# Two cross-attention and expert layers on one core: z rows stored as fp16 halves and brought into columns by DMA transposes, one joined q/k weight in the second attention, and the second expert weights split earlier

## The chip, the cores and the metric

The kernel runs on one core of a Trainium2 chip. The metric is the device time of one execution in microseconds (us). TensorE is called PE here, VectorE DVE, ScalarE ACT, GpSimd POOL and SyncE SP, as in the profile.

## What is computed

The state x is 16 batches of 256 tokens of 256 values, f32. Four parts each add to it, times tanh of a gate:

- first attention: layernorm of x as 256 latents; four heads of 64; keys and values come from a context (256 rows of 192 values) and from the latents;
- first experts: logits over 8 experts, the best two by softmax, each with silu(z W1) * (z W2) W3 and an inner width of 352, and one shared expert for all tokens;
- second attention: one head, `q = z Wq + bq`, `k = ctx Wk + bk`, `v = ctx Wv + bv`, scores `q kT`, softmax, `P v`;
- second experts: best one of 8, gelu, inner width 512, biases, the result times the gate's probability.

z is the layernorm of x at each of these places. The expert products are made from fp16 halves: a number is its fp16 rounding (high) plus the fp16 rounding of what is left (low), and three products (high with high, high with low, low with high) stand for one in f32.

## The kernel before

The phases stand one after the other, with a barrier between them: constants, first attention (about 31 to 440 us), its routing tail and a table of tiles (to 482), expert stage 0 (482 to 838), second attention (838 to 1081), its table (to 1100), expert stage 1 (1100 to the end).

**Attention phases.** Each engine has its own instruction stream; they meet by semaphores alone. `over_batches` (L247) writes a software pipeline: in step n an engine works on batch n+1 ("front"), n ("core"), n-1 ("tail") and n-2 (routing). The order inside a step is written out by hand, and an engine never leaves it: an instruction that waits holds up all behind it on that engine. Some steps at both ends are written out, the rest are a loop.

`Route` (L261) is the part of both attention phases that prepares the experts. DVE makes `z_tokens` (`vector_z`, L335) into one of two buffers, PE turns it (`pe_turn`, L346), ACT copies the columns (`act_cols`), PE makes logits and prefix sums, DVE chooses experts and slots (`vector_choose`, `vector_slots`; the last result is `slot_idx`, L446), and POOL sends each row to its slot in HBM by indirect DMAs of 128 rows (`pool_scatter`, L457, L464): four for a batch in the first attention, two in the second. In the first attention SP also stores the plain rows for the shared expert. A row is 1024 bytes of f32 z; in the second attention it carries the probability, the token number and the token's x behind z.

POOL's step in the second attention (L1625) is: `pool_rstd(n-1)` (L318, L319), `fetch(n+3)` (four gathers of expert results, L1515), `rstd(n+2)` (L1620, L1621), `pool_scatter(n-2)`. DVE uses the second rstd for `x_norm` (`pre_norm`, L1770), and PE's step begins with turning that (`turn`, L1846). Steps n = 2 to 12 have both a fetch and a scatter.

PE's step there is: turn x and context of n+1, scores of n, logits of n-2, projection of q and then of k of n+1 (`project_qk`, L1858; the k part is L1868), turning of probabilities, projection of v, prefix sums, turning of z of n-1, products of n. ACT adds the biases of q and k (`bias_q_or_k`, L1653).

**Weights.** `Weights` (L180) brings the expert weights of a layer in by parts, one for each batch step of the attention before it: SP loads 256 or 352 KB and more, ACT makes the high halves (`high`, L223), DVE the low ones (`low`, L231; the `v_low` rows of the profile are its work in the second attention, L234).

**Expert stages.** Stage 0 has 103 tiles of 128 rows (71 routed, 32 shared), stage 1 has 39. `over_tiles` (L1274) writes the pipeline: in step s PE makes the first products of tile s, turns tile s+1 of z (`z_cols`, L1403) and the hidden rows of s-1 (L1410), and makes y of s-2 (L1419). The z rows come as f32 by one plain SP load of 128 KB (L1351), issued three tiles ahead into four buffers. ACT rounds the turned columns to `z_high` (L1431) and DVE subtracts for `z_low` (L1487); the first products (L1393) wait for `z_low`. ACT and DVE further make the hidden rows and their halves. In stage 0 SP stores y; in stage 1 POOL scatters it to the output.

Of the kernel before, what the change touches and what calls it, by code (L numbers as in the profile page):

```python
# [15 lines left out]
P = 128  # L16
# [11 lines left out]
F1 = 512  # L28
REG = NTOK + P
# [43 lines left out]
def program(nc, a, out):  # L73
    root = ExitStack()
    with root:
# [34 lines left out]
        with ExitStack() as l0:  # L110
# [7 lines left out]
            end_of_phase(nc, g)  # L118
            phase_experts(nc, a, g, 0)
            end_of_phase(nc, g)  # L120
        with ExitStack() as l1:
            g["v1h"] = sb("v1_high", [P, KC * E * F1], F16, l1)
            g["v1l"] = sb("v1_low", [P, KC * E * F1], F16, l1)
            g["v2h"] = sb("v2_high", [P, 4 * E * C], F16, l1)
            g["v2l"] = sb("v2_low", [P, 4 * E * C], F16, l1)
            g["b1"] = sb("b1_rows", [P, E * F1], F32, l1)
            g["b2"] = sb("b2_rows", [P, E * C], F32, l1)
# [52 lines left out]
class Weights:  # L180
# [5 lines left out]
    def __init__(self, nc, g, a, c, layer):  # L186
        self.g, self.layer = g, layer
        if layer == 0:
            self.parts, self.first_rows, self.second_rows = 2 * (E + 1), a["w13"], a["w2"]
            self.F, self.EW, names = 2 * F0, E + 1, ("w13h", "w13l", "w2h", "w2l")  # L190
        else:
            self.parts, self.first_rows, self.second_rows = 2 * E, a["v1"], a["v2"]
            self.F, self.EW, names = F1, E, ("v1h", "v1l", "v2h", "v2l")
        self.first_rows = self.first_rows.rearrange("e c f -> (e c) f")
        self.second_rows = self.second_rows.rearrange("e f c -> (e f) c")
        self.high1, self.low1, self.high2, self.low2 = (g[x][:] for x in names)
        self.stage1 = [c.enter_context(nc.sbuf_tensor(f"w{layer}_stage_first{p}", [P, self.F], F32)) for p in range(2)]
        self.stage2 = [c.enter_context(nc.sbuf_tensor(f"w{layer}_stage_second{p}", [P, 2 * C], F32)) for p in range(2)]
        sem = lambda n: phase_semaphore(nc, g, f"w{layer}_{n}")
# [3 lines left out]
        if layer == 0:  # L203
            self.second = [[(0, P, 0, 0)], [(P, P, 1, 0), (2 * P, F0 - 2 * P, 2, 1)]]
        else:
            self.second = [[(0, P, 0, 0), (P, P, 1, 1)], [(2 * P, P, 2, 0), (3 * P, P, 3, 1)]]
# [8 lines left out]
    def load(self, sp, j, q):  # L215
        sp.wait_ge(self.low_done, count(j - 1))
        inner = F0 if self.layer == 0 else F1
        sp.dma_start(self.stage1[q][:], self.first_rows[ds(j * P, P), :]).then_inc(self.landed[q], 16)
        for row, rows, _, place in self.second[q]:
            sp.dma_start(self.stage2[q][0:rows, place * C:(place + 1) * C],  # L220
                         self.second_rows[ds((j - q) * (inner // 2) + row, rows), :]).then_inc(self.landed[q], 16)
# [9 lines left out]
    def low(self, v, j, q):  # L231
# [3 lines left out]
        ins.then_inc(self.low_done, 1)  # L235

# [24 lines left out]
class Route:  # L261
# [6 lines left out]
    def __init__(self, nc, g, c, tag, K, SL, PR, RUN, rows, wg):  # L268
# [19 lines left out]
        self.z = [sb(f"z_tokens{p}", [P, T, rows.shape[1]]) for p in range(2)]  # L288
# [4 lines left out]
        self.z_turned = sem("z_turned")  # L293
        if K == 1:
# [40 lines left out]
    def vector_z(self, v, n, p, x, shared):  # L335
# [3 lines left out]
        v.wait_ge(self.scattered[p], count((n - p) * (8 * self.K * T)))  # L339
        if shared:  # L340
            v.wait_ge(self.stored[p], count((n - p) * 8))
        for t in range(T):
            ins = v.tensor_scalar(self.z[p][:, t, 0:C], x[:, t, :], self.mv[:, t, 0:1], self.rstd[:, t:t + 1], ALU.subtract, ALU.mult)
        ins.then_inc(self.z_ready, 1)

    def pe_turn(self, pe, n, p, bank):  # L346
        pe.wait_ge(self.z_ready, n + 1)
        for k in range(KC):
            for t in range(T):
                ins = pe.transpose(bank[:, k, t * P:(t + 1) * P], self.z[p][:, t, k * P:(k + 1) * P], self.g["ident"][:])  # L350
# [63 lines left out]
    def vector_slots(self, v, n, p, prefix, beside=None):  # L414
# [13 lines left out]
        if self.K == 1:  # L428
            ch.mark(v.tensor_scalar(self.z[p][:, :, SCALE], self.sum[:], self.g["gate"][:, 3:4], None, ALU.mult))
            ch.mark(v.tensor_copy(self.z[p][:, :, NUMBER], self.number[:]))  # L430
# [19 lines left out]
    def act_tokens(self, act, n, p):  # L450
# [4 lines left out]
        act.activation(self.z[p][:, :, TOKEN:TOKEN + C], self.g["XR"][:, ds(n * T, T), :], ACT.Copy).then_inc(self.tokens_copied, 1)  # L455
# [104 lines left out]
def phase_attn0(nc, a, g):  # L560

    NS1 = DC - P
    with ExitStack() as c:
# [33 lines left out]
        xo = sb("x_mid", [P, T, C])  # L597
# [10 lines left out]
        weights, table, dummies_padded = Weights(nc, g, a, c, 0), Table(nc, g, c, 0, [x[:].rearrange("p j s -> p (j s)") for x in (pm[0], pm[1], ksq)]), sem("dummies_padded")  # L608
# [25 lines left out]
        with nc.Block() as block:  # L634
            @block.sync
            def _(sp):
# [6 lines left out]
                def store(m, p):  # L643
                    sp.wait_ge(rt.z_ready, m + 1)
                    sp.dma_start(g["z0"][ds(m * S + SHARED, S), :].rearrange("(t p) c -> p t c", p=P), rt.z[p][:]).then_inc(rt.stored[p], 16)

                def step(n, q):
# [4 lines left out]
                    if isinstance(n, int) and n == -3:  # L652
                        for dst, src in loads:
                            sp.dma_start(dst, src).then_inc(consts_in, 16)
                    if within(n - 1, B):
# [1316 lines left out]
```

## Time and profile before

| | |
|---|---|
| time, median of 3 runs | 1256.4 us (1250.9 to 1256.54) |
| the profiled execution | 1255.76 us, span 1253.9 us |
| busy: PE, DVE, ACT, POOL | 1113.0 (89%), 765.0 (61%), 600.4 (48%), 412.0 (33%) us |
| mean granted clock of PE | 0.94 of full speed |

The share of each engine is a mean over phases with different limits. PE is the busiest, but the records of weight loads overlap it, and in POOL's busy time are the indirect DMAs that it issues. A row of windows has, in order: the window, its length, busy time and (instructions) of PE, of PE's weight loads, of DVE, ACT and POOL, the granted clock, the busy share of the DMA engines, and GB/s. A row of a timeline has start, busy time, engine, line, operation, output and inputs; in brackets stand the engine's idle time just before it and what ended that.

### The profile page before, as it was taken

What the parts mean: (1) busy time and instruction counts of PE and PEld (TensorE: products, weight loads), DVE (VectorE), ACT (ScalarE), POOL (GpSimd) and SP (SyncE); (2) the same over time, 40 slices, a digit from 0 to 9 for tenths busy, and PEclk for the clock granted to TensorE, in tenths of its full rate; (3) what the DMA queues carried; (4) which work ended last, traced back from release to release, by engine and by line L of the source; (5) the groups of instructions that cost most, each with busy time, mean ns of one, the idle gap of its engine ahead of it and who ended that gap; (6) DMA issues with size and microseconds to landing.
All of it is one profiled execution on the core that took longest, in us unless ns stands there. A gap on an engine that the chain in (4) does not pass through costs nothing. (4 is left out here: it accounts for less than half of the span.)

```text
span 1253.9 us, 31159 instructions
## 1 busy us (share of the span) xinstructions
PE 1113.0 (89%) x8451; PEld 859.0 (69%) x8452; DVE 765.0 (61%) x2494; ACT 600.4 (48%) x1400; POOL 412.0 (33%) x485
## 2 busy tenths in 40 slices
PE   3999999999999944999999999965999998289996
PEld 2677777777777733777777777744777777256664
DVE  5467777777777662344444444434788887447775
ACT  3466665666566521444444444422555555033442
POOL 3345555556465430000000000004566662212222
PEclk9799999999999866999999999986999999579999
DMA  4123121311221112222222222225764541433341
GB/s 132 32 66 101 57 69 56 101 63 55 67 82 50 45 64 71 74 79 79 79 79 79 78 79 78 79 81 156 269 192 155 165 151 59 118 89 106 109 110 52
DMA packets 94382, 116.21 MB, mean 93 GB/s; under 512 B 12479, under 2 KB 80049, under 8 KB 94066
## 3 DMA queue, kind: packets, MB, share of 16 engines
q1 hardware_dynamic: 82594, 84.50, 22.1%
q0 software_dynamic: 10576, 29.41, 6.7%
q10 hardware_dynamic: 1152, 1.58, 0.5%
q8 instruction: 28, 0.46, 0.1%
q14 instruction: 32, 0.26, 0.1%
HBM read 70.43 MB, written 45.92 MB: 93 GB/s over the span
## 5 line engine op out<-in xcount | busy, mean ns | idle before, releaser
L1487 DVE TENSOR_TENSOR e_z_low<-e_z_cols,e_z_high 128x256 f16<-128x256 f32 x142 | 59.9, 422 | 209.5 <-ACT e_z_high L1431 209.2
L1431 ACT ACTIVATE e_z_high<-e_z_cols 128x256 f16<-128x256 f32 x142 | 54.5, 384 | 254.8 <-PE e_z_cols L1403 254.8
L1128 PE MATMUL a_out<-a_v_ones,a_probs 128*128 128x65 f32 x1024 | 140.6, 281 | 0.0
L1128 PEld LDWEIGHTS a_out<-a_v_ones,a_probs 128*128 128x128 f32 x1024 | 126.8, 195 | 15.3 <-issue 15.3
L464 POOL DMA_INDIRECT z_rows<-r_z_tokens,r_slot_idx x96 | 96.4, 1004 | 75.8 <-ACT r_z_tokens L455 35.7
L1608 POOL IOTA a_first_numbers<- 128x2 int32 x1 | 0.1, 125 | 367.7 <-POOLq L69 367.7
L772 ACT ACTIVATE a_probs<-a_scores,a_latent_bias,a_k_scales 128x256 f32<-128x256 f32 x128 | 65.3, 561 | 94.5 <-PE a_scores L1114 57.1
L1497 DVE TENSOR_TENSOR e_hidden_low<-e_hidden_cols,e_hidden_high 128x384 f16<-128x384 f32 (+1 forms) x142 | 83.6, 588 | 36.8 <-ACT e_hidden_high L1446 36.7
L1393 PE MATMUL e_first<-w_high,e_z_high 128*128 x412 | 96.6, 316 | 4.2 <-DVE e_z_low L1487 3.5
L1393 PE MATMUL e_first<-w_low,e_z_high 128*128 x412 | 96.3, 316 | 0.0
L1393 PE MATMUL e_first<-w_high,e_z_low 128*128 x412 | 96.3, 316 | 0.0
L1403 PE MATMUL e_z_cols<-ident,e_z_rows 128*128 128x128 f32 x284 | 55.6, 278 | 39.5 <-DMA e_z_rows<-z_rows 39.5
L1419 PE MATMUL e_y<-w_high,e_hidden_high 128*128 (+1 forms) x309 | 84.4, 273 | 2.1 <-DVE e_hidden_low L1497 1.8
L1419 PE MATMUL e_y<-w_high,e_hidden_low 128*128 (+1 forms) x309 | 84.1, 272 | 0.0
L1419 PE MATMUL e_y<-w_low,e_hidden_high 128*128 (+1 forms) x309 | 84.0, 272 | 0.0
L1373 POOL DMA_INDIRECT out_x<-e_y_rows,e_token_numbers x39 | 38.4, 984 | 126.7 <-DVE e_y_rows L1510 123.4
L1515 POOL DMA_INDIRECT a_y_chosen<-y_rows,a_slots x64 | 66.2, 1034 | 39.6 <-issue 22.9
L1403 PEld LDWEIGHTS e_z_cols<-ident,e_z_rows 128*128 128x128 f32 x284 | 40.4, 144 | 54.2 <-DMA e_z_rows<-z_rows 39.7
L1410 PE MATMUL e_hidden_cols<-ident,e_hidden 128*128 128x128 f32 (+1 forms) x465 | 74.5, 274 | 1.3 <-ACT e_hidden L1441 0.9
L695 POOL TENSOR_TENSOR a_k_scales<-a_square_sums,minus_half 128x16 f32<-128x16 f32 x16 | 46.4, 2901 | 87.7 <-DVEq L924 87.7
L1446 ACT ACTIVATE e_hidden_high<-e_hidden_cols 128x384 f16<-128x384 f32 (+1 forms) x142 | 73.8, 520 | 0.9 <-PE e_hidden_cols L1410 0.9
L772 ACT ACTIVATE a_probs<-a_scores,a_mask_bias,a_k_scales 128x256 f32<-128x256 f32 x128 | 65.4, 568 | 8.5 <-PE a_scores L1114 5.1
(339 smaller groups left out, 3083.3 us busy)
## 6 DMA issues: line engine op xcount, KB each, us to landing
e_z_rows<-z_rows SPq DMA_DIRECT2D x142, 128.0 KB, 2.0
y_rows<-e_y_rows SPq DMA_DIRECT2D x103, 128.0 KB, 1.7
w_stage_first<-in_w SPq DMA_DIRECT2D x18, 352.0 KB
a_ctx_in<-in_ctx SPq DMA_DIRECT2D x32, 192.0 KB, 3.7
e_token_rows<-z_rows SPq DMA_DIRECT2D x39, 129.0 KB, 2.1
residual<-in_x SPq DMA_DIRECT2D x16, 256.0 KB, 3.6
z_rows<-r_z_tokens SPq DMA_DIRECT2D x16, 256.0 KB, 2.2
a_y_shared<-y_rows SPq DMA_DIRECT2D x16, 256.0 KB, 2.8
```

Of the source, the lines that this page charges most:

```text
L464: pool.indirect_dma_start(self.rows, bass.IndirectOffsetOnAxis(ap=self.idx[p][:, k, t:t + 1], axis=0), self.z[p][:, t, :], None).then_inc( ...
L772: act.activation(pm[x][:, jt, :], SC[x][:, 0:S], ACT.Exp, bias=b, scale=rr[p][:, jt * 4 + h:jt * 4 + h + 1]).then_inc(exps, 1)
L1128: ins = pe.matmul(O[t][:, h * (D + 1):(h + 1) * (D + 1)], pm[x][:, jt, t * P:(t + 1) * P], va[p][:, jt, h, :], start=i + x == 0, stop=i + ...
L1393: ins = pe.matmul(GU[p][f][:, 0:F], x[p][:, k, :], w[:, ds(off, F)], start=(k == 0 and x is xh and w is wh), stop=(k == KC - 1 and x is xl))
L1403: ins = pe.transpose(ZT[:, k * P:(k + 1) * P], zs[z][:, k * P:(k + 1) * P], g["ident"][:])
L1410: ins = pe.transpose(HT[p % NH][0:m, n * P:(n + 1) * P], hs[p][:, o:o + m], g["ident"][:])
L1419: ins = pe.matmul(Y[p][:, 0:C], x[p][0:m, n, :], w[0:m, ds(e * C + n * EW * C, C)], start=(n == 0 and x is hh and w is uh), stop=(n == NCH ...
L1431: act.activation(xh[p][:].rearrange("p k s -> p (k s)"), ZT[:, 0:KC * P], ACT.Copy).then_inc(zhigh, 1)
L1446: act.activation(hh[p][:].rearrange("p k s -> p (k s)"), HT[p % NH][:, 0:HW], ACT.Copy).then_inc(hhigh, 1)
L1487: v.tensor_tensor(xl[p][:].rearrange("p k s -> p (k s)"), ZT[:, 0:KC * P], xh[p][:].rearrange("p k s -> p (k s)"), ALU.subtract).then_inc( ...
L1497: v.tensor_tensor(hl[p][:].rearrange("p k s -> p (k s)"), HT[p % NH][:, 0:HW], hh[p][:].rearrange("p k s -> p (k s)"), ALU.subtract).then_ ...
L1515: pool.indirect_dma_start(dst, None, rows, bass.IndirectOffsetOnAxis(ap=idx[:, k, t:t + 1], axis=0)).then_inc(done, 16)
```

## The change

1. z is made in one f32 buffer. ACT makes the fp16 high half (`act_z_high`, two instructions of 128x256 for a batch), POOL the low half (`pool_z_low`, two of 128x256). Both go into `zrow`, 1024 bytes for a row as before, and the scatters and stores send that. `act_z_high` stands behind the last exps in the first attention, behind `act_cols` in the second; `pool_z_low` is the last of POOL's step. `vector_z` waits for the turn and the low half of the batch before, `pool_scatter` and the store wait for the low half. In the first attention SP's store goes behind the load of weights.
2. In both expert stages SP's load becomes a DMA transpose of 128 rows x 512 fp16 into four 128x128 blocks. PE's turning, ACT's `z_high` and DVE's `z_low` go; the first products wait for the landing alone, and the load waits for the first products of four tiles before.
3. The weights of stage 1 are split in stage 0, 64 pieces of 128x256, one with each of the tiles 12 to 75 (SP a load of 128 KB, ACT one instruction, DVE one); `over_tiles` gets a second loop and more written-out steps. The second attention has none of it any more.
4. At the start of the second attention PE makes Wq WkT and its column for bk once. In the loop the k projection and its biases go; q's columns are 128 + 65 rows, scores contract them with the context's columns, which have two buffers now.
5. The first attention loses one buffer (`x_mid`); the work is the same.

```diff
-    def vector_z(self, v, n, p, x, shared):
+    def vector_z(self, v, n, x):
         v.wait_ge(self.rstd_ready, n + 1)
-        v.wait_ge(self.scattered[p], count((n - p) * (8 * self.K * T)))
+        v.wait_ge(self.z_turned, count(n))
+        v.wait_ge(self.z_low, count(n))
+        for t in range(T):
+            ins = v.tensor_scalar(self.z[:, t, :], x[:, t, :], self.mv[:, t, 0:1], self.rstd[:, t:t + 1], ALU.subtract, ALU.mult)
...
+    def act_z_high(self, act, n, p, shared):
+        act.wait_ge(self.scattered[p], count((n - p) * (8 * self.K * T)))
...
+        act.wait_ge(self.z_ready, n + 1)
         for t in range(T):
+            ins = act.activation(self.zhalf[p][t][:, 0:C], self.z[:, t, :], ACT.Copy)
+        ins.then_inc(self.z_high, 1)
+    def pool_z_low(self, pool, n, p):
+        pool.wait_ge(self.z_high, n + 1)
+        for t in range(T):
+            ins = pool.tensor_tensor(self.zhalf[p][t][:, C:2 * C], self.z[:, t, :], self.zhalf[p][t][:, 0:C], ALU.subtract)
+        ins.then_inc(self.z_low, 1)
...
     def pool_scatter(self, pool, n, p):
+        pool.wait_ge(self.z_low, n + 1)
...
-                                        self.z[p][:, t, :], None).then_inc(self.scattered[p], 16)
+                                        self.zrow[p][:, t, :], None).then_inc(self.scattered[p], 16)
...
+class NextWeights:
+    FIRST, PIECES, AHEAD = 12, 8 * E, 3
+    def load(self, sp, i, q):
+        if not isinstance(i, int) or i >= 4:
+            sp.wait_ge(self.low_done, i - 2)
...
+        sp.dma_start(self.stage[q][:], rows).then_inc(self.landed[q], 16)
+    def high(self, act, i, q):
+        act.wait_ge(self.landed[q], (i - q) * 4 + 16)
+        act.activation(high[:, ds(at, C)], self.stage[q][:], ACT.Copy, scale=WSCALE).then_inc(self.high_done, 1)
+    def low(self, v, i, q):
+        v.wait_ge(self.high_done, i + 1)
+        v.scalar_tensor_tensor(low[:, ds(at, C)], self.stage[q][:], WSCALE, high[:, ds(at, C)], ALU.mult, ALU.subtract).then_inc(self.low_done, 1)
...
                     if within(i, tiles):
-                        sp.wait_ge(turned, count(i - NZ + 1))
-                        sp.dma_start(zs[p][:], zd[ds(r, P), 0:C]).then_inc(landed[p], 16)
+                        sp.wait_ge(first_done, count(i - NZ + 1))
+                        sp.dma_start_transpose(zT[p][:], zd[ds(r, P), 0:C].bitcast(F16)).then_inc(landed[p], 16)
...
-                        pe.wait_ge(zlow, i + 1)
+                        pe.wait_ge(landed[z], (i - z) * (16 // NZ) + 16)
...
-                            ins = pe.transpose(ZT[:, k * P:(k + 1) * P], zs[z][:, k * P:(k + 1) * P], g["ident"][:])
...
-                        act.activation(xh[p][:].rearrange("p k s -> p (k s)"), ZT[:, 0:KC * P], ACT.Copy).then_inc(zhigh, 1)
...
-                        v.tensor_tensor(xl[p][:].rearrange("p k s -> p (k s)"), ZT[:, 0:KC * P], xh[p][:].rearrange("p k s -> p (k s)"), ALU.subtract).then_inc(zlow, 1)
...
-                    if within(n + 3, weights.parts):
-                        weights.load(sp, n + 3, 1 - q)
...
                     if within(n - 2, B):
                         rt.pool_scatter(pool, n - 2, q)
+                    if within(n - 1, B):
+                        rt.pool_z_low(pool, n - 1, 1 - q)
...
-                    for i in range(KC):
-                        for k, (o, w) in enumerate(CTX_CHUNKS):
-                            ins = pe.matmul(PJ[1][:, i * S:(i + 1) * S], wk[0:w, k, i * P:(i + 1) * P], cT[0:w, k, :], start=k == 0, stop=k == 1)
...
+                        for k, (o, w) in enumerate(D_CHUNKS):
+                            ins = pe.matmul(SC[:, t * S:(t + 1) * S], qT[p][0:w, k, t * P:(t + 1) * P], cT[p][0:w, k, :], start=k == 0, stop=k == KC - 1)
```

## Rows read from the trace of the kernel before

**Rows 1.** Windows: expert stage 0, second attention, expert stage 1.

```profile
564.00:596.00 32.00, 32.00 (x253) 25.40 (x252) 13.07 (x29) 14.43 (x39) 0.00 (x0) 1.00 0.25 78
...
972.00:1003.00 31.00, 30.44 (x167) 23.68 (x167) 27.60 (x114) 16.09 (x45) 20.89 (x24) 1.00 0.51 163
...
1160.00:1191.00 31.00, 30.25 (x213) 21.54 (x212) 21.69 (x54) 13.30 (x27) 8.86 (x9) 1.00 0.39 110
```

**Rows 2.** Timeline of PE, expert stage 0, one tile; start, busy, instruction.

```profile
599.56 0.46 PE L1393 MATMUL e_first<-w_high,e_z_high 128*128 x2
...
601.35 0.38 PE L1403 MATMUL e_z_cols<-ident,e_z_rows 128*128 128x128 f32 x2
...
601.57 0.49 PE L1410 MATMUL e_hidden_cols<-ident,e_hidden 128*128 128x128 f32 x3
...
602.88 0.46 PE L1393 MATMUL e_first<-w_high,e_z_high 128*128 x2
```

**Rows 3.** Timeline of PE, first tiles of both expert stages; idle before in brackets.

```profile
484.53 0.76 PE L1393 MATMUL e_first<-w_high,e_z_high 128*128 x2 [1.27 <-DVE e_z_low L1487]
...
489.94 0.77 PE L1393 MATMUL e_first<-w_high,e_z_high 128*128 x2 [1.29 <-DVE e_z_low L1487]
...
1102.35 0.61 PE L1393 MATMUL e_first<-v_high,e_z_high 128*128 x1 [1.65 <-DVE e_z_low L1487]
```

**Rows 4.** DMA issues: tensors, count, KB each, median us to landing.

```profile
e_z_rows<-z_rows SPq DMA_DIRECT2D x142, 128.0 KB, 2.0
...
a_ctx_in<-in_ctx SPq DMA_DIRECT2D x32, 192.0 KB, 3.7
```

**Rows 5.** Timeline of DVE, expert stage 1, one tile.

```profile
1180.23 0.68 DVE L1480 SCALAR_TENSOR_TENSOR e_act_out<-e_first,b_rows 128x512 f32<-128x512 f32 x1
...
1182.22 0.69 DVE L1497 TENSOR_TENSOR e_hidden_low<-e_hidden_cols,e_hidden_high 128x512 f16<-128x512 f32 x1 [0.98 <-ACT e_hidden_high L1446]
...
1183.68 0.68 DVE L1480 SCALAR_TENSOR_TENSOR e_act_out<-e_first,b_rows 128x512 f32<-128x512 f32 x1
```

**Rows 6.** Timeline of DVE, second attention, end of one batch step.

```profile
996.27 0.69 DVE L234 SCALAR_TENSOR_TENSOR v_low<-w_stage_first,v_high 128x512 f32 x1
...
997.55 0.16 DVE L1734 COPY a_probs_chosen<-probs 128x4 f32 x1
```

**Rows 7.** Timeline of PE, second attention: k projection, next turn.

```profile
986.80 2.48 PE L1868 MATMUL a_proj<-a_ctx_cols,a_wk 128*128 128x256 f32 x8
...
994.38 0.65 PE L1851 MATMUL a_turn<-ident,a_x_norm 128*128 128x128 f32 x4 [0.45 <-DVE a_x_norm L1770]
```

**Rows 8.** Timeline of POOL, second attention, one batch step.

```profile
996.55 0.46 POOL L318 TENSOR_TENSOR r_rstd<-r_mean_var,eps_tile 128x2 f32<-128x2 f32 x1
...
998.91 1.34 POOL L1515 DMA_INDIRECT a_y_chosen<-y_rows,a_slots  x1 [1.03 <-issue]
...
1004.36 0.71 POOL L1621 TENSOR_TENSOR a_rstd<-a_rstd,minus_half 128x2 f32<-128x2 f32 x1
...
1006.73 1.05 POOL L464 DMA_INDIRECT z_rows<-r_z_tokens,r_slot_idx  x1 [1.67 <-ACT r_z_tokens L455]
...
1009.21 0.61 POOL L318 TENSOR_TENSOR r_rstd<-r_mean_var,eps_tile 128x2 f32<-128x2 f32 x1
```

**Rows 9.** Groups by line and shape, POOL, first attention, 235 to 439 us.

```profile
L464 POOL DMA_INDIRECT z_rows<-r_z_tokens,r_slot_idx x32 | 31.6, 988 | 8.7 <-issue 8.7
...
L695 POOL TENSOR_TENSOR a_k_scales<-a_square_sums,minus_half 128x16 f32<-128x16 f32 x8 | 23.2, 2901 | 44.0 <-DVEq L924 44.0
...
L685 POOL TENSOR_TENSOR a_k_squares<-a_k_cols 128x512 f32<-128x512 f32 x15 | 15.6, 1040 | 1.9 <-POOL r_rstd L319 1.9
```

**Rows 10.** Windows of 4 us at the end of the first attention.

```profile
424.00:428.00 4.00, 3.21 (x21) 2.16 (x18) 2.19 (x12) 1.90 (x4) 3.08 (x4) 0.62 0.60 212
428.00:432.00 4.00, 4.00 (x23) 3.21 (x23) 1.54 (x7) 1.65 (x4) 0.65 (x1) 0.50 0.17 60
432.00:436.00 4.00, 4.00 (x24) 2.58 (x22) 1.56 (x3) 1.02 (x3) 0.00 (x0) 0.60 0.00 0
```

More of the change, by code:

```diff
@@ L28 @@
 F1 = 512
+F1P = F1 + 16
 REG = NTOK + P
@@ L287, in __init__ @@
         self.idx = [sb(f"slot_idx{p}", [P, K, T], I32) for p in range(2)]
-        self.z = [sb(f"z_tokens{p}", [P, T, rows.shape[1]]) for p in range(2)]
+        self.z = sb("z_tokens", [P, T, C])
+        self.zrow = [sb(f"z_halves{p}", [P, T, rows.shape[1]]) for p in range(2)]
+        halves = lambda p: [self.zrow[p][:, t, 0:C].bitcast(F16) for t in range(T)]
+        self.zhalf = [halves(p) for p in range(2)]
         self.zT = sb("z_cols", [P, KC, S])
@@ L293, in __init__ @@
         self.z_turned = sem("z_turned")
+        self.z_high, self.z_low = sem("z_high"), sem("z_low")
         if K == 1:
@@ L1271, in ahead, with over_tiles, run @@
             self.of(1)
-def over_tiles(eng, step, n, experts=None):
-    def run(s, q):
+def over_tiles(eng, step, n, experts=None, next_weights=None):
+    def run(s, q, filling):
         if experts:
             experts.s, experts.q = s, q
-        step(s, q)
-    for s in range(-3, 8):
-        run(s, s % 4)
-    if experts:
-        experts.enter_loop(8)
-    end = 8 + (n - 3 - 8) // 4 * 4
-    with eng.Fori(8, end - 3, 4) as s:
-        for q in range(4):
-            run(s + q, q)
-    if experts:
-        experts.leave_loop()
-    for s in range(end, n + 3):
-        run(s, s % 4)
+        step(s, q, filling)
+    if next_weights:
+        first, end = next_weights.FIRST, next_weights.FIRST + next_weights.PIECES
+        loops = [(first, end - 4, True), (end, end + (n - 3 - end) // 4 * 4, False)]
+    else:
+        loops = [(8, 8 + (n - 3 - 8) // 4 * 4, False)]
+    at = -3
+    for first, end, filling in loops:
+        for s in range(at, first):
+            run(s, s % 4, True)
+        if experts:
+            experts.enter_loop(first)
+        with eng.Fori(first, end - 3, 4) as s:
+            for q in range(4):
+                run(s + q, q, filling)
+        if experts:
+            experts.leave_loop()
+        at = end
+    for s in range(at, n + 3):
+        run(s, s % 4, True)
 def phase_experts(nc, a, g, layer, out=None):
@@ L1318, in phase_experts @@
         NY = 2 if layer == 0 else 4
-        zs = [sb(f"z_rows{p}", [P, C]) for p in range(NZ)]
-        tokens = [sb(f"token_rows{p}", [P, W1 - TOKEN]) for p in range(NZ)]
-        xh = [sb(f"z_high{p}", [P, KC, P], F16) for p in range(2)]
-        xl = [sb(f"z_low{p}", [P, KC, P], F16) for p in range(2)]
+        zT = [sb(f"z_cols{p}", [P, 2 * KC, P], F16) for p in range(NZ)]
+        xh, xl = [z[:, 0:KC, :] for z in zT], [z[:, KC:2 * KC, :] for z in zT]
+        tokens = [sb(f"token_rows{p}", [P, W1 - TOKEN]) for p in range(NZ)] if layer else None
         act_out = sb("act_out", [P, F])
@@ L1360, in step @@
                         sp.dma_start(yd[ds(i * P, P), :], ys[p][:]).then_inc(stored[p], 16)
-                over_tiles(sp, step, tiles)
+                    if next_piece(s, AHEAD, filling):
+                        next_weights.load(sp, s - FIRST + AHEAD, (q + AHEAD) % 4)
+                over_tiles(sp, step, tiles, None, next_weights)
                 for p in range(NY):
@@ L1451, in step @@
                         act.activation(ys[p][:], Y[p][:, 0:C], ACT.Copy, scale=1.0 / WSCALE).then_inc(y_out, 1)
-                over_tiles(act, step, tiles)
+                    if next_piece(s, 0, filling):
+                        next_weights.high(act, s - FIRST, q)
+                over_tiles(act, step, tiles, None, next_weights)
             @block.vector
@@ L1595, in step @@
                         load_ctx(n + 3, 1 - q)
-                    if within(n + 3, weights.parts):
-                        weights.load(sp, n + 3, 1 - q)
                 over_batches(sp, -4, step, B - 5)
@@ L1638, in step @@
                         rt.pool_scatter(pool, n - 2, q)
+                    if within(n - 1, B):
+                        rt.pool_z_low(pool, n - 1, 1 - q)
                 over_batches(pool, -4, step, B - 5)
@@ L1697, in step @@
                         copy_v(n + 1, 1 - q)
-                        bias_q_or_k(n + 1, 1 - q, 1)
-                    if not early and within(n + 1, weights.parts):
-                        weights.high(act, n + 1, 1 - q)
                 over_batches(act, -1, step)
@@ L1821, in step @@
                         x3(n)
-                    if within(n + 1, weights.parts):
-                        weights.low(v, n + 1, 1 - q)
                     if isinstance(n, int) and n == -3:
@@ L1833, in _, with join_weights @@
                 ident = g["ident"]
-                pe.wait_ge(ones_ready, 1)
+                pe.wait_ge(ones_ready, 2)
                 pe.wait_ge(consts_in, n_consts)
+                def join_weights():
+                    for k in range(KC):
+                        for h in range(KC):
+                            ins = pe.matmul(WB[:, k * (DC + 1):(k + 1) * (DC + 1)], wq[:, h, k * P:(k + 1) * P], wk[:, h, :], start=h == 0, stop=h == KC - 1)
+                    ins.then_inc(joined, 1)
+                    for k, (o, w) in enumerate(D_CHUNKS):
+                        for h in range(KC):
+                            ins = pe.matmul(PJ[0:w, k:k + 1], wk[:, h, o:o + w], bq[:, h:h + 1], start=h == 0, stop=h == KC - 1)
+                    ins.then_inc(joined, 1)
                 def router():
```

244 lines of the change are left out of this document (130 added, 114 removed).

## The prediction

> **What bounds the kernel now.** I read the windows first, since each phase has a limit of its own. In expert stage 0 PE is busy for 32.00 of 32 us at full clock, while ACT and DVE have less than half of the time and the DMA engines a quarter [rows 1]. The timeline then shows PE's tile from the first products at 599.56 to the next at 602.88, so 3.32 us, with no idle time in it [rows 2]: whatever PE loses there the stage loses, 103 times. Expert stage 1 looks alike by its windows, but its timeline shows a ring of ACT and DVE: DVE's `act_out` at 1180.23, ACT's gelu and `hidden_high` behind it, then DVE's `hidden_low` at 1182.22, for which DVE has stood idle 0.98 us, and the next `act_out` at 1183.68 [rows 5]. The period is 3.45 us, and PE only follows. In the second attention PE has 30.44 of 31 us and DVE 27.60 [rows 1]. There a batch step is 12.66 us (the same POOL instruction at 996.55 and 1009.21 [rows 8]); PE waits 0.45 us of it for DVE's `x_norm` [rows 7], so PE and DVE are both at their limit, and POOL, which seems free by its share, has an order of its own that nearly fills the step [rows 8].
>
> **Expert stage 0.** PE's turning of z goes. It costs from its start at 601.35 to that of the hidden rows at 601.57, 0.22 us a tile [rows 2], not the 0.38 us of the row, since matmuls overlap: 3.32 becomes 3.10, and 103 x 0.22 = -22.7 us. What is late next? ACT lost `z_high` and DVE `z_low`, and get a weight piece of the same 128x256 size in 64 of the tiles, so their shares of 14.43 and 13.07 in 32 us [rows 1] stay; nothing of theirs is near 3.10. SP gets one more issue a tile, and the load behind it waits for pieces two tiles back. The DMA engines get 128 KB more beside 256 KB, so about 0.25 x 1.5 x 3.32 / 3.10 = 0.40 busy. All that hides if the transposes keep up: each must come in at one per 3.10 us, and is issued three tiles, over 9 us, ahead.
>
> The trace has no DMA transpose. The nearest rows are the plain load of the same bytes, 2.0 us to landing, and the slowest of the frequent loads, 192 KB in 3.7 us [rows 4]; plain loads overlap one another. From below, a transpose costs what the load does and nothing shows. From above, if transposes ran one at a time and each took 3.7 us, the tile would be 3.70 us. I take the first, as it moves the same bytes. At the start of the stage the first products wait 1.27 and 1.29 us for the halves of the first two tiles [rows 3]: -2.5 us.
>
> The plain rows here say that 128 KB is 2.0 us. The Trainium skill, "VectorE: DVE Perf Modes", The three transpose paths, speaks against the edit: it gives 1309 ns to a DMA transpose of 128x128 and 390 ns to TensorE's, and its rules prefer TensorE where the result may lie in PSUM. No row here can bear that out; four blocks one behind the other would be 5.2 us a tile by that page, an estimate, and the stage would grow by some 220 us over my forecast. "Advanced Engine Details and Errata", X-Bar Transpose, says instead that these transposes are as fast as regular DMAs, by which my sum stands.
>
> **Expert stage 1.** The same three operations go, but none is in the ring: `z_low` lies in DVE's idle 0.98 us [rows 5]. So the steady part gains nothing (bounds: 0, and -8.6 us if PE's 0.22 counted in each of 39 tiles). The start gains the wait of 1.65 us [rows 3] and some of the second tile's: -2.
>
> **Second attention.** DVE loses `v_low`, 996.27 to 997.55, 1.28 us [rows 6]: 12.66 becomes about 11.4. PE loses the k projection, about 2.4 us [rows 7]: 12.66 - 0.45 - 2.4 = 9.8. ACT loses two biases and the high halves and gets two instructions for z. POOL gets `pool_z_low`, and there the gain stops. Its step now: rstd 996.55 to 997.89; a gap of 1.03; four gathers from 998.91; the second rstd to 1005.07; a gap of 1.67; two scatters from 1006.73 to about 1009.1 [rows 8]. The gaps are waits for DVE's slots; if POOL is late, they shrink. How far, the first attention shows: scatters whose slots are ready come after gaps of 8.7 us over 32, 0.27 each [rows 9]. So POOL's own work is 12.66 - (1.03 - 0.27) - (1.67 - 0.27) = 10.5 us. If the gaps are the price of an indirect DMA behind arithmetic, it is 11.9 with only 0.7 of them gone.
>
> The price of `pool_z_low` itself is not in the trace. Nearest is POOL's product of 128x512 in 1040 ns [rows 9]; half as many elements is 0.5, and the small first rstd takes 0.46 [rows 8]. Bounds 0.3 to 1.04, I take 0.6, 1.2 for a batch. POOL's step is then 11.7 to 13.1. I take 11.9, nearer to the end that rests on the ready scatters. The eleven steps that both fetch and scatter gain 12.6 - 11.9 = 0.7 each, -7.7. Steps 13 and 14, which fetch nothing, are PE's and gain its k, 2 x 2.3 = -4.6. The first steps lose DVE's part and much DMA traffic: -2. Sum -14.3. The joined weight at the start takes four PE products and a few copies, less than the wait for the first gathers that hides it; without that cover it costs 2 us.
>
> **First attention.** ACT gets two instructions of 128x256, about 0.8 us a batch, behind its exps; POOL's pair fits in its idle 44.0 us over 8 batches, 5.5 each [rows 9]. It stands behind the scatter, ahead of the next rstd, which is needed much later. The store is now queued on SP behind a load of weights; it is needed only at the end of the phase. PE is the limit here and its work stays. Bounds -1 to +10 (all of ACT's time on the path, 16 x 0.8 less what is idle); I take +3, some of the exps being late.
>
> **Sum.** -22.7 - 2.5 - 2 - 14.3 + 3 = -38.5 us on the profiled execution's 1255.8, which is 0.6 below the median of the runs: 1217 us.
>
> **Rivals.** (a) POOL binds the second attention and PE's clock falls. POOL's step at 13.1 costs 1.2 x 11 = +13, so 1230. PE would then wait about 3 us in a step (2 by my forecast). The clock fell after such a pause in the first attention's end: in the window where PE was busy for 3.21 of 4 us it went to 0.62, the next to 0.50, that is 1.2 instead of 2.4 GHz, then 0.60 [rows 10], which lost 4 x (0.38 + 0.50 + 0.40) = 5.1 us of work. A step that loses this takes PE 9.8 + 5.1 = 14.9 us, has no pause, and the next is fast again: every second step +1.8, six times, +11: 1241. Against it: with pauses of 0.45 us the clock stayed at 1.00 [rows 1, 7].
>
> (b) Slower: the transposes are late. At 3.7 us a tile, stage 0 takes 103 x (3.70 - 3.10) = +62, stage 1 39 x (3.70 - 3.45) = +10, so 1289. It decides at 38.5 / 103 = 0.37 above 3.10: from some 3.47 us for each transfer on, the change loses. For it: no transfer of this kind is in the trace. Against it: a quarter of the DMA engines' time is in use [rows 1], and the load has a lead of 9 us. The page's 1309 ns for a block would be its far end, four of them a tile, and its chance of 0.04 is within that of (b).
>
> (c) The change does not shorten PE's tile, because the new wait for the landing, or the hidden rows' halves, come late by the same 0.22 us: 1217 + 23 = 1240.
>
> (d) POOL hides the new pair and DVE sets 11.4 us: 11 x 0.5 less, 1211.
>
> **How the numbers follow.** Chances: forecast 0.42 (its own range 1207 to 1228), (a) 0.23, (b) 0.14, (c) 0.10, (d) 0.07, and 0.04 that several small losses together end within 0.5% of before. A measurement of this kernel can tell no less than 0.5%, 6.3 us, from no change, so faster is below 1250 and slower above 1263. Faster: 0.42 + 0.07 + 0.21 of (a) + 0.08 of (c) = 0.78; same 0.07; slower 0.15, nearly all (b). The range leaves out the far part of (b) and a little below (d): 1202 to 1270.
>
> **What would show it.** Right: stage 0 with tiles of 3.10 us and PE without idle time; the second attention's steps at 11.9 us with PE waiting about 2 us for `x_norm` and POOL without its long gap ahead of the scatters; stage 1 still at 3.45 us. Wrong: first products that wait for a landing in the steady part (b); a granted clock below 1.00 within the second attention (a); `e_y` or `hidden_cols` waiting (c); steps of the first attention over 25.5 us (204 us for the 8 of [rows 9]).

## The result, and the profile after

The changed kernel takes 1236.6 us (median of four runs, 1230.5 to 1239.5) against 1255.8 before: a ratio of 0.986, interval 0.983 to 0.989. So it is faster by 19 us, 1.4%, clear of the noise by the interval, where 38.5 were forecast. The profiled execution has a span of 1234.3 us against 1253.9. Lengths of the phases, each read from the starts of the named instructions in the two timelines; the forecast column puts each term of the prediction to the phase in which it falls:

| us | before | after | difference | forecast |
|---|---|---|---|---|
| start to the first products of stage 0 | 484.5 | 485.5 | +0.9 | +1.7 |
| to those of its last tile (103 tiles) | 345.0 | 331.9 | -13.2 | -23.7 |
| to the first maximum of the second attention | 43.8 | 42.5 | -1.3 | -2 |
| to its last maximum | 187.1 | 184.0 | -3.1 | -12.3 |
| to the first products of stage 1 | 41.9 | 42.0 | +0.1 | -1.7 |
| to those of its last tile | 136.1 | 132.2 | -3.8 | -0.3 |
| to the end | 15.5 | 16.3 | +0.8 | 0 |

Two phases kept most of what was to go: expert stage 0 (10.5 us) and the second attention (9.2 us). How much such a phase varies by itself, the kernels below show: up to the first products of stage 0 all are the same, and this takes them 483.9 to 488.9 us, so the first row tells nothing; the second attention takes 183.4 to 184.9 us in the two further profiles that leave it as it is here. Windows of the kernel after, columns as in [rows 1]: stage 0 early and later, the second attention, stage 1.

```profile
540.00:570.00 30.00, 30.00 (x235) 23.37 (x234) 14.39 (x30) 14.98 (x38) 0.00 (x0) 1.00 0.42 115
600.00:630.00 30.00, 29.16 (x217) 21.47 (x216) 13.29 (x27) 14.10 (x36) 0.00 (x0) 1.00 0.44 118
960.00:990.00 30.00, 25.39 (x143) 20.27 (x141) 25.06 (x103) 13.98 (x40) 21.16 (x27) 0.94 0.32 107
1140.00:1170.00 30.00, 28.26 (x193) 18.93 (x192) 18.32 (x42) 10.04 (x18) 8.82 (x9) 1.00 0.41 109
```

In stage 0 PE is busy all the time at first, as before, but later it stands still for 0.84 of 30 us, by the records, whose ends are modelled; in the second attention it is busy for 25.39 of 30 only, and its clock is granted at 0.94 on the mean of this window. DVE has 25.06 of 30 there, 84% against 89% in [rows 1]: that is 10.7 us a step where it had 11.3, though the 1.28 us of `v_low` are gone.

Timeline of PE in the middle of stage 0, starts of tiles: the period of [rows 2] is 3.28, 3.40 and 3.14 us here, and the first of these tiles waits for its transpose.

```profile
596.44 0.47 PE L1468 MATMUL e_first<-w_high,e_z_cols 128*128 x2 [0.33 <-DMA e_z_cols<-z_rows]
...
599.72 0.47 PE L1468 MATMUL e_first<-w_high,e_z_cols 128*128 x2
...
603.12 0.47 PE L1468 MATMUL e_first<-w_high,e_z_cols 128*128 x2
...
606.26 0.47 PE L1468 MATMUL e_first<-w_high,e_z_cols 128*128 x2
```

The starts of all tiles show where this is. From the fourth to the 29th they come 3.10 us apart, as forecast, with one exception (3.33); from 573.05 to 727.15 there are 46 tiles with a mean of 3.35; then come two of 4.8 and 4.3; and from 736 on they are 3.10 again. The weight pieces run from about 518 to 729 us. Against tiles of 3.10 the stretch from 573 to 739 loses some 14 us. From the list of waits, 575 to 724 us:

```profile
PE e_first L1468 <- DMA e_z_cols<-z_rows: 3.1, 13, 0.3
```

So the first products wait 13 times for a landing; the weight loads ahead of them stand still too (41 times, 15.0 us), with no releaser that the profile shows.

Timeline of SP in that stretch, one tile:

```profile
660.46 1.22 SPq L1424 DMA_TRANSPOSE e_z_cols<-z_rows  x1
661.96 0.35 SPq L1433 DMA_DIRECT2D y_rows<-e_y_rows  x1
662.60 0.35 SPq L259 DMA_DIRECT2D w_stage<-in_v  x1
663.85 1.21 SPq L1424 DMA_TRANSPOSE e_z_cols<-z_rows  x1
```

A transpose holds SP for 1.21 us, where the plain load took 0.33 us; store and load follow, with register work between them, and the next transpose starts 3.39 us after the first. In the list of waits SP waits for nothing between 590 and 720 us, and its records there, with the register instructions, which the timeline leaves out, have no gap above 0.13 us between them. So SP is full, and the 0.9 us ahead of each transpose is register work, 0.28 us of it the load of the tile's row number. It is full long before the tiles are late: from 526 us on the transposes start 3.35 us apart on the mean, and the time from a transpose's issue to its first products falls from 7.6 us, before the pieces begin, to 2.9 at 573 us, and stays at 2.6 to 3.1 up to 724. Who waits for SP is in the list of waits of stage 0:

```profile
ACT e_y_rows L1514 <- DMA y_rows<-e_y_rows: 42.1, 46, 1.9
```

ACT may not overwrite a y buffer until SP's store of two tiles before has landed; 46 times that is late.

The second attention: DVE at the turn of a step, and POOL around it.

```profile
958.85 0.68 DVE L1847 TENSOR_REDUCE a_minus_max<-a_scores 128x2 f32<-128x512 f32 x1
...
970.11 0.36 DVE L1805 COPY a_probs_chosen<-probs 128x4 f32 x1
970.38 1.37 DVE L1806 COPY a_slots<-slots 128x4 int32 x1
971.67 0.68 DVE L1847 TENSOR_REDUCE a_minus_max<-a_scores 128x2 f32<-128x512 f32 x1
```

```profile
960.87 1.03 POOL L1579 DMA_INDIRECT a_y_chosen<-y_rows,a_slots  x1 [1.03 <-issue]
...
968.06 1.05 POOL L521 DMA_INDIRECT z_rows<-r_z_halves,r_slot_idx  x1 [1.24 <-ACT r_z_halves L511]
...
970.42 1.30 POOL L398 TENSOR_TENSOR r_z_halves<-r_z_tokens,r_z_halves 128x256 f16<-128x256 f32 x2
...
973.69 1.03 POOL L1579 DMA_INDIRECT a_y_chosen<-y_rows,a_slots  x1 [1.03 <-issue]
```

DVE's step is 12.82 us (the maxima at 958.85 and 971.67) though `v_low` is gone. Two copies of four columns, 0.16 us each before (the second row of [rows 6] is one), now take 0.36 and 1.37 us, and the second ends with POOL's pair for the low halves, 970.42 to 971.72. POOL's gap ahead of the gathers is 1.03 us as in [rows 8], the one ahead of the scatters 1.24.

### The profile page after: what moved, and what is told of

Same layout as the page of the kernel before. It is cut to its first block and busy times, and to the rows that moved or that the text cites. A ratio compares the mean times of both kernels' runs of the same rounds, so it can differ in the third digit from the quotient of the medians.

```text
span 1234.3 us, 29884 instructions
## 1 busy us (share of the span) xinstructions
PE 1056.1 (86%) x8055; PEld 808.2 (65%) x8056; DVE 744.4 (60%) x2369; ACT 570.7 (46%) x1309; POOL 449.7 (36%) x549
## 3 DMA queue, kind: packets, MB, share of 16 engines
q1 hardware_dynamic: 141746, 84.51, 24.3%
## 5 line engine op out<-in xcount | busy, mean ns | idle before, releaser
L1468 PE MATMUL e_first<-w_high,e_z_cols 128*128 x824 | 175.2, 315 | 27.3 <-DMA e_z_cols<-z_rows 25.1
L1554 DVE SCALAR_TENSOR_TENSOR e_hidden<-e_first,e_act_out 128x352 f32<-128x352 f32 x103 | 54.0, 524 | 142.3 <-ACT e_act_out L1500 142.3
L1468 PEld LDWEIGHTS e_first<-w_high,e_z_cols 128*128 128x128 f16 x824 | 80.6, 98 | 74.1 <-issue 39.0
L521 POOL DMA_INDIRECT z_rows<-r_z_halves,r_slot_idx x96 | 96.3, 1003 | 65.6 <-issue 33.8
L1500 ACT ACTIVATE e_act_out<-e_first 128x352 f32<-128x352 f32 x103 | 47.8, 464 | 113.5 <-PE e_first L1468 112.8
L1468 PE MATMUL e_first<-w_low,e_z_cols 128*128 x412 | 95.7, 314 | 0.0
L1468 PE MATMUL e_first<-v_high,e_z_cols 128*128 x156 | 54.3, 391 | 23.5 <-DMA e_z_cols<-z_rows 21.9
L1514 ACT ACTIVATE e_y_rows<-e_y 128x256 f32<-128x256 f32 x103 | 39.6, 384 | 72.9 <-DMA y_rows<-e_y_rows 42.1
L1477 PEld LDWEIGHTS e_hidden_cols<-ident,e_hidden 128*128 128x128 f32 (+1 forms) x465 | 57.9, 138 | 17.6 <-issue 4.0
```

The costliest lines, as they stand in the source:

```text
L1468: ins = pe.matmul(GU[p][f][:, 0:F], x[z][:, k, :], w[:, ds(off, F)], start=(k == 0 and x is xh and w is wh), stop=(k == KC - 1 and x is xl))
L1477: ins = pe.transpose(HT[p % NH][0:m, n * P:(n + 1) * P], hs[p][:, o:o + m], g["ident"][:])
L1500: act.activation(act_out[:], GU[p][0][:, 0:F], ACT.Silu, scale=1.0 / WSCALE).then_inc(act_done, 1)
L1554: v.scalar_tensor_tensor(hs[p][:], GU[p][1][:, 0:F], 1.0 / WSCALE, act_out[:], ALU.mult, ALU.mult).then_inc(hidden_done, 1)
```

## The experiments

**Expert stage 0: loads issued by POOL.** In the changed kernel, out of SP's step and into a loop of POOL's own:

```diff
-                    if next_piece(s, AHEAD, filling):
-                        next_weights.load(sp, s - FIRST + AHEAD, (q + AHEAD) % 4)
...
+                def fill(s, q, filling):
+                    if next_piece(s, AHEAD, filling):
...
+                        next_weights.load(pool, s - FIRST + AHEAD, (q + AHEAD) % 4)
+                if layer == 0:
+                    over_tiles(pool, fill, tiles, None, next_weights)
```

> The changed kernel, with the 64 loads of weight pieces in expert stage 0 issued by POOL (which is idle there) and not by SP; the bytes are the same. Theory Q: between 573 and 736 us SP's instruction stream is full (transpose 1.21 us, store 0.41, load 0.35, with what lies between 3.33 us a tile), and it sets the tile. Then all tiles take 3.10 us, the time from the first products of the first tile to those of the last falls from 331.9 to about 317 us, and the whole kernel is some 14 us shorter. Rival B: the DMA engines, or the transposes beside two other transfers, are the limit. Then the tiles stay at about 3.3 us and nothing is gained.

It took 1219.0 us. From the fourth on the tiles are 3.10 us apart but for three (3.21, 3.44 and 3.66) and the last; from the first tile's products to the last one's it is 318.3 us, 26.7 less than before. Window and timeline of this kernel:

```profile
640.00:672.00 32.00, 32.00 (x249) 24.68 (x247) 15.15 (x32) 16.22 (x42) 5.39 (x10) 1.00 0.51 130
```

```profile
647.97 0.54 POOL L259 DMA_DIRECT2D w_stage<-in_v  x1 [2.57 <-DVE v_low L270]
...
648.16 1.21 SPq L1424 DMA_TRANSPOSE e_z_cols<-z_rows  x1
...
649.65 0.34 SPq L1433 DMA_DIRECT2D y_rows<-e_y_rows  x1
...
650.89 1.22 SPq L1424 DMA_TRANSPOSE e_z_cols<-z_rows  x1
```

PE is busy for 32.00 of 32 us, and the DMA engines are busier (0.51) than when the tiles were late (0.44). So rival B is out: the transposes keep a rate of one in 3.10 us beside two other transfers, and it was SP's side that was full. A transpose still holds SP for 1.21 us here, so that time does not come from SP's being full. The four kernels with the loads on POOL have 318.0 to 318.6 us for this phase, the seven with SP's loads 329.9 to 332.5.

The same kernel timed:

> The loads of weight pieces on POOL alone, timed: 1219 to 1222 us, ratio about 0.972. Theory Q gives 1236.6 - 15 = 1221.6. If the single run was a lucky one, it is nearer to 1236.

1222.8 us (1220.1 to 1228.0), ratio 0.975, interval 0.971 to 0.978. The profiled execution here is the one at 1228.0; it is the same kernel as the first run's, and 5 of the 9 us that it has more lie ahead of stage 0. So single runs below are read by the lengths of their phases.

**The second attention: who does the low half.** Out of POOL's step, to the end of DVE's:

```diff
-                    if within(n - 1, B):
-                        rt.pool_z_low(pool, n - 1, 1 - q)
...
+                    if tail:
+                        rt.pool_z_low(v, m, 1 - q)
```

> The changed kernel, with the low half of z in the second attention made by DVE at the end of its step, not by POOL. Theory L: DVE is held while POOL does its pair (DVE's copy of the slots takes 1.37 us there, 0.16 without); freed of that, and with 0.75 us for the pair, DVE's step goes from 12.8 to about 12.1 us. Theory P: POOL's own order with its two gaps of about 1.0 and 1.2 us is the limit; without the pair POOL needs 11.6 us, and the step is DVE's 12.1 too. Both: 6 to 8 us shorter in the second attention.

Steps of 12.2 and 12.5 us in turn; some take 13.3, where the granted clock falls. From the first to the last maximum it is 180.9 us, 3.1 less than in the kernel after; the phase gained half or less of the 6 to 8 us that both theories said. DVE's pair takes 0.73 us, and its copies are back at 0.16.

**Another form of the held instructions.**

```diff
-                    v.tensor_copy(pr[p][:], g["PR0"][:, ds(m * T, T), :])
+                    v.tensor_tensor(pr[p][:], g["PR0"][:, ds(m * T, T), :], g["PR0"][:, ds(m * T, T), :], ALU.max)
...
```

> The changed kernel, with DVE's two small copies at the start of its step in the second attention (probabilities and slots) written as a maximum of the source with itself; POOL keeps its pair. Theory L: only some forms of DVE instructions are held up by POOL's pair; if two-input ones are not, the two take 0.16 us each beside it, DVE's step falls to about 11.5 and the whole step to 11.8 to 12.3 us. If they are held too, nothing changes. Theory P: the gather of POOL starts no earlier, the step stays at 12.8 us in either case, though the two instructions are short.

Nothing changed: steps of 12.3 to 13.5 us, 184.2 in all, which either theory allows. DVE and POOL of this kernel:

```profile
957.04 0.60 DVE L1805 TENSOR_TENSOR a_probs_chosen<-probs 128x4 f32 x1 [0.43 <-issue]
957.57 0.70 DVE L1807 TENSOR_TENSOR a_slots<-slots 128x4 int32 x1
```

```profile
956.94 1.30 POOL L398 TENSOR_TENSOR r_z_halves<-r_z_tokens,r_z_halves 128x256 f16<-128x256 f32 x2
```

The two-input form is held as well: 0.60 and 0.70 us, ending with the pair at 958.24.

**The pair at another place.**

```diff
+                    if within(n - 1, B):
+                        rt.pool_z_low(pool, n - 1, 1 - q)
                     if within(n - 2, B):
                         rt.pool_scatter(pool, n - 2, q)
-                    if within(n - 1, B):
-                        rt.pool_z_low(pool, n - 1, 1 - q)
```

> The changed kernel, with POOL's pair for the low half of z in the second attention ahead of its scatter and not behind it, in the gap of 1.24 us in which POOL waits for DVE's slots. Theory P: the gap is filled, and POOL's step falls by about 1.2 to 11.6 us, some 12 us less in all. Theory L: DVE is held at another place (the normalisation of x, 0.74 us, lies there), its step stays within 0.4 us of 12.8, or grows, since the slots that POOL waits for come late too.

Steps of 12.7 to 13.3 us, 185.8 in all: theory L. What is held moved with the pair. The groups of DVE, where the row of `x_norm` has 410 ns in the kernel after:

```profile
L1841 DVE TENSOR_SCALAR a_x_norm<-residual,a_mean_var,a_rstd 128x256 f32 x16 | 10.2, 680 | 1.8 <-DVE r_slot_idx L502 1.8
```

```profile
919.04 1.25 POOL L1579 DMA_INDIRECT a_y_chosen<-y_rows,a_slots  x1 [1.03 <-issue]
...
925.83 1.34 POOL L398 TENSOR_TENSOR r_z_halves<-r_z_tokens,r_z_halves 128x256 f16<-128x256 f32 x2 [0.63 <-ACT r_z_halves L391]
927.35 1.05 POOL L521 DMA_INDIRECT z_rows<-r_z_halves,r_slot_idx  x1 [0.18 <-issue]
```

The scatter follows the pair after 0.18 us, the gather still has 1.03 us ahead of it, though its slots were ready: that gap belongs to the gather, the scatter's was mostly a wait.

**No pair at all.** This kernel leaves the low halves of z at zero:

```diff
-                        rt.pool_z_low(pool, n - 1, 1 - q)
+                        pool.wait_ge(rt.z_high, n)
+                        pool.tensor_tensor(rt.zhalf[1 - q][0][:, C:C + 8], rt.z[:, 0, 0:8], rt.zhalf[1 - q][0][:, 0:8], ALU.subtract).then_inc(rt.z_low, 1)
+                for p in range(2):
+                    for t in range(T):
+                        pool.memset(rt.zhalf[p][t][:, C:2 * C], 0.0)
```

> The changed kernel without POOL's pair in the second attention (the low halves of z are left at zero for expert stage 1; one POOL instruction of 8 columns stands in its place). Theory L: DVE's two copies take 0.16 us each again, its step falls by about 1.1 us to 11.5 to 11.7 us, and the phase from the first maximum to the last by some 12 us. If POOL's gathers and scatters bind by themselves, the step stays above 12.2 us.

This spoke against theory L as it stood: the copies are near 0.16 us again (0.17 to 0.2 on the mean), but the step is 12.2 to 12.5 us at full clock, and 180.2 in all: 3.8 less than in the kernel after where some 12 were expected, and hardly less than with the pair on DVE. DVE now waits, and the waits close a ring. DVE and PE of this kernel:

```profile
943.07 0.69 DVE L1851 TENSOR_REDUCE a_minus_max<-a_scores 128x2 f32<-128x512 f32 x1 [0.73 <-PE a_scores L1961]
...
951.53 0.73 DVE L1845 TENSOR_SCALAR a_x_norm<-residual,a_mean_var,a_rstd 128x256 f32 x2 [0.23 <-DVE r_slot_idx L502]
...
955.26 0.69 DVE L1851 TENSOR_REDUCE a_minus_max<-a_scores 128x2 f32<-128x512 f32 x1 [0.19 <-PE a_scores L1961]
```

```profile
952.40 0.65 PE L1934 MATMUL a_turn<-ident,a_x_norm 128*128 128x128 f32 x4 [0.78 <-DVE a_x_norm L1845]
...
953.32 1.90 PE L1961 MATMUL a_scores<-a_ctx_cols,a_q_cols 128*128 128x256 f32 x8
```

From the maxima at 943.07 DVE works its order down to `x_norm` at 951.53; PE turns that at 952.40, and only then, in its own order, makes the scores of the batch before; the next maxima are at 955.26, 12.19 us after the first. In some steps between, PE's turn is released by ACT's `a_v_tokens` instead, which ends at nearly the same time (940.01 us, `x_norm` at 939.94).

`v_low` stood on DVE in the part of the ring that is PE's. So does what is held beside the pair. PE's scores and DVE's maxima behind them, first in the kernel before, then in the kernel after:

```profile
995.30 1.89 PE L1883 MATMUL a_scores<-a_k_cols,a_q_cols 128*128 128x256 f32 x8
...
997.69 0.69 DVE L1776 TENSOR_REDUCE a_minus_max<-a_scores 128x2 f32<-128x512 f32 x1
```

```profile
969.09 1.90 PE L1957 MATMUL a_scores<-a_ctx_cols,a_q_cols 128*128 128x256 f32 x8
...
971.67 0.68 DVE L1847 TENSOR_REDUCE a_minus_max<-a_scores 128x2 f32<-128x512 f32 x1
```

Before, the scores end at 997.19 and the maxima come 0.50 us later: of the 1.28 us of `v_low` no more than that could be gained without touching PE's order. After, the scores end at 970.99 and the maxima come 0.68 us later, behind the held copies: no more than that is the price of the pair in this step.

**Scores ahead of the turning.** In PE's step, on the kernel without the pair:

```diff
+                    if core:
+                        score(n, q)
                     if front:
                         turn(n + 1, 1 - q)
...
-                    if core:
-                        score(n, q)
```

> The kernel without POOL's pair in the second attention (low halves of z left at zero), and in PE's step the scores of batch n ahead of the turning of batch n+1. Theory R: without the pair the step of 12.2 us is a ring: DVE from the maxima of the scores to the normalisation of x (8.5 + 0.7 us), then PE's turning of it and, only behind that, the scores (2.9 us), then the maxima again. With the scores first the ring is open, and the step falls to DVE's own sum, 11.4 to 11.6 us. If something else binds, the step stays at 12.2 to 12.5.

The phase takes 175.0 us, 5.2 less. In the kernel without the pair the list of DVE's waits from 895 to 985 us has this line, and here there is none on the scores:

```profile
DVE a_minus_max L1851 <- PE a_scores L1961: 3.1, 6, 0.7
```

So the ring is open, as theory R says. But of the steps in the middle only four reach the 11.4 to 11.6 us forecast, 11.45 to 11.48; five others at full clock take 11.84 to 12.57, and one with a lower clock 12.89. In these DVE stands still for other things, 0.4 us ahead of its copies and for POOL's rstd (`a_rstd`) among them; what binds there was not followed.

**PE's work made more.**

```diff
-                    for i, (o, w) in enumerate(D_CHUNKS):
+                    for i, (o, w) in [*enumerate(D_CHUNKS), *enumerate(D_CHUNKS)]:
```

> The changed kernel, with the q projection of the second attention made twice into the same place: 1.8 us more of PE in each step, about three quarters of the k projection that the joined weight took away. If PE has the slack that its waits of 1.5 and 0.7 us in a step of 12.8 show, the time stays within 3 us, and the joined weight gave nothing here. If PE is on the path, 16 x 1.8 = 29 us are added.

1235.7 us, and 184.6 from the first to the last maximum, against 184.0: 16 x 1.8 us of PE cost nothing that this can tell, where PE on the path would have cost 29. Windows of this kernel:

```profile
906.00:956.00 50.00, 45.93 (x269) 37.99 (x269) 42.70 (x170) 23.22 (x64) 35.19 (x46) 1.00 0.35 117
956.00:1006.00 50.00, 46.16 (x274) 38.38 (x273) 43.59 (x170) 22.44 (x62) 35.60 (x48) 1.00 0.36 116
```

PE is busier by 3 to 5 us in 50 than in the kernel after, and the clock, below 1.00 in three of the 15 steps there, is granted in full here; a little of PE's added work may be paid by that.

**Both remedies.** Loads on POOL and the low half on DVE:

> The changed kernel, with both: the loads of weight pieces issued by POOL in expert stage 0, and the low half of z made by DVE in the second attention. If the two losses are independent, the time is that of the first alone, 1219 us, less the 3 to 5 us that the second gave alone: 1214 to 1216 us, a ratio to the kernel before of about 0.969. If the second gained only by chance of the clock, it stays at 1219.

1221.5 us (1215.7 to 1233.5), ratio 0.976, interval 0.972 to 0.980. That is above the 1214 to 1216 expected. The interval overlaps that of the loads alone; the second attention has the 180 us of the second remedy, but the total can't tell them apart.

With the scores ahead of the turning as well, which takes the ring away:

> The kernel with loads on POOL and the low half on DVE, and with the scores ahead of the turning in PE's step. Theory R: the step falls from 12.2 or 12.5 to DVE's sum with the pair, 12.05 us: 2 to 5 us less than the 1221 (fast runs 1216) of the same kernel without it, a ratio to the kernel before of 0.970 to 0.973. If DVE alone bound it there, nothing changes.

1211.7 us (1208.0 to 1216.1), ratio 0.970, interval 0.968 to 0.973. All steps from 889 to 985 us are 11.88 to 12.00 us, near the 12.05 expected, and the phase from the first to the last maximum is 174.6 us, 12.5 less than before and 5.4 less than with both remedies alone; a part of this is the clock, which fell in two steps there (13.3 us instead of 12.1 to 12.5) and in none here. Windows of stage 0 and of the second attention:

```profile
560.00:592.00 32.00, 32.00 (x251) 24.94 (x249) 15.02 (x31) 16.43 (x42) 6.01 (x11) 1.00 0.50 126
910.00:942.00 32.00, 27.82 (x168) 23.66 (x166) 28.61 (x117) 16.22 (x44) 21.99 (x26) 1.00 0.35 115
```

The clock is full in both. This is the best version here: 39 us below the kernel before in the runs beside it (1251.1), twice the change's own 19.

## Why the prediction was wrong

- **Stage 0, the step that failed first.** "SP gets one more issue a tile ... All that hides if the transposes keep up." The transposes did keep up; SP did not. I counted the transfers and put what the issues take of SP at nothing, as with a plain load's 0.33 us. A transpose's measured 1.21 us, and with store, load and register work SP's tile is 3.35 us. The lead on which I relied, over 9 us, was 7.6 us and was used up at 0.25 us a tile. PE's 0.22 us, read from [rows 2], was right: tiles are 3.10 us where no pieces are loaded, and everywhere with the loads on POOL. The term is -23.7 forecast, -13.2 measured, and -26.7 with SP free of the pieces; some 4 us of this come from the first and last tiles.
- **The second attention, the step that failed as a mechanism.** "DVE loses `v_low` ... 12.66 becomes about 11.4 ... and there the gain stops" at POOL. POOL's pair measured 1.3 us, near the 1.2 of the estimate, and I looked for its cost in POOL's order alone. It lies in DVE's: DVE is held while the pair runs, as the runs on place, form and absence show. POOL's order did not set the step: filling its gap gained nothing. The term is -12.3 forecast, -3.1 measured. The measured 12.8 us lies between my 11.9 and the 13.1 of rival (a), but by neither's reason.
- **Under it, a bound that I had not seen.** Even without the pair the step was 12.2 us. [rows 7] had the sign of it: PE's turn waits for `x_norm`, and PE's order puts the scores behind the turn, so the maxima can't come earlier than both; with `v_low` there they came 0.50 us behind the scores, and no more was to be had. I read the 0.45 us as PE and DVE both at their limit and took each one's sum; the ring through the two is longer than either. PE's other work is off this ring: of the 2.4 us a step that the joined weight took from PE, 1.8 put back cost nothing that can be measured, so it gave next to nothing here.
- **POOL's gaps.** That both shrink was wrong for one: the gather's 1.03 us stays with ready slots. The scatter's is 1.06 to 1.24 us in the kernel after, and went to 0.18, near the 0.27 of [rows 9], where the pair stands ahead of it.
- **Rivals.** (a) came true in the second half of its text: the clock does fall in steps with PE's pauses, three of 15, to 0.97 on the mean of the phase. What a fall costs can't be told in the kernel after, where steps with one take 13.0 to 13.1 us and steps at full clock up to 13.4; with the low half on DVE it is 13.3 against 12.2 to 12.5, so near 0.9 us each, not 1.8. (b) is out, though its sign, first products that wait for a landing, was seen: the issues were late, not the transfers. (c) came true for 46 tiles, by SP's queue, which it had not named. The measured 1236.6 us lie near the 1240 and 1241 of (c) and (a), but that is chance: neither made the time. By the Trainium skill, "VectorE: DVE Perf Modes", The three transpose paths, I worked out 5.2 us a tile, an estimate; one in 3.10 us was measured with the DMA engines 0.51 busy, so four times its 1309 ns is not the rate here.
- **What was right.** Stage 1 nearly keeps its period: the mean of four tiles is 3.47 us after, 3.51 before, with PE idle for 1.74 of 30 us; that the ring of [rows 5] binds it was not tried. It gained 3.7 us, where 2 were forecast, but in its tiles (3.8 against 0.3) and not at its start (0.1 lost against 1.7). The first attention came out within what its phase varies by itself.

There is a rule for this hold that I had not weighed. The rows: from 890 to 1000 us DVE's two copies take 1.04 us together on the mean beside the pair, and 0.32 with the low half on DVE. The Trainium skill, "SBUF — State Buffer", SBUF: two separate sides, says that DVE and GpSimd share one pair of ports, which the first to start holds for its whole instruction; on DVE's side this concerns instructions in a two-port mode and, against a GpSimd instruction that reads SBUF, those with two inputs there. The run with the other form agrees for the second kind, with 0.60 and 0.70 us instead of 0.16; that the ports are the cause no run here shows by itself.

## What to carry to other kernels

Price an edit on every queue that issues it: a transfer that hides on the DMA engines can still fill the instruction stream that starts it, and a slow start shows only when the lead of the buffers is used up, here after 18 tiles. Before giving an engine's slack to new work, ask which engine it may hold up; work on an idle POOL was paid by DVE. And where two engines both look full, follow one batch round through them: an order that makes one wait for the other's next batch is a bound of its own, and turning two steps of PE's order round was worth 5 us, more than taking the pair from POOL (3 to 4 us) or 1.8 us a step from PE (nothing).

## What the runs showed of the hardware

- A DMA transpose of 128 x 512 fp16 held SP for 1.21 us; the plain load of the same bytes 0.33. Beside a store and a plain load a tile, transposes came one in 3.10 us with the DMA engines 0.51 busy. The first transpose of stage 0 was in use 2.8 us after its issue (482.7 to 485.5), and the program has about 59,000 more packets on that queue (141,746 against 82,594), some 417 for each transpose.
- A plain load of 128 KB issued by POOL took 0.54 us of it and landed after 2.6 us, against 0.35 and 2.1 from SP.
- DVE instructions of 0.16 us took up to 1.37 us beside POOL's pair (the kernel after), and `x_norm` 680 ns on the mean instead of 410 (the pair ahead of the scatter).
- The first of a step's indirect gathers had 0.91 to 1.04 us ahead of it in every kernel here; the scatter 0.18 us when nothing was waited for.
- With PE pausing 1.4 to 1.6 us and 0.7 us in a step of the kernel after (busy for 25.39 of 30 us) the clock fell in three of 15 steps; it was granted in full with q made twice (45.93 of 50 us) and in the last kernel (27.82 of 32 us).
